# A mixed stack of attention and expert layers on one core: values of the local layers by DRAM, norm factors on GpSimd, heads scored side by side

## The reference, cut to what matters

```python
def attn_layer(x, Wqkv, qs, ksc, Wo):          # x: (16, 256, 128), 16 heads of 64
    q, k, v = jnp.split(x @ Wqkv, 3, -1)        # per head
    q = l2norm(q) * qs
    k = l2norm(k) * ksc
    q = q * cos * scale + rotate_half(q) * sin * scale
    k = k * cos * inv + rotate_half(k) * sin * inv
    out = local_attention(q, k, v)              # windows of 32 see themselves and the one before
    return out @ Wo
def ffn_layer(x, g, bln, W1, b1, W2, b2):
    a, gate = jnp.split((layernorm(x) * g + bln) @ W1 + b1, 2, -1)
    return a * gelu(gate) @ W2 + b2
for i in range(6):
    x = attn_layer(shift_tokens(x), ...) + x
    x = ffn_layer(shift_tokens(x), ...) + x
```

## Time and profile before

| | us |
|---|---|
| median of three runs | 7244.83 (7240.41 to 7246.15) |
| the profiled execution | 7247.5 |
| its span | 7245.8 |
| TensorE busy | 6522.4 (90%) |
| VectorE busy | 4927.7 (68%) |
| ScalarE busy | 4182.4 (58%) |
| GpSimd busy | 2901.3 (40%) |

### The profile page before, as it was taken

One profiled execution on the slowest core, in us unless ns is written; L12 is line 12 of the kernel. 1 busy time (PEld: TensorE's weight loads), 2 busy tenths in 40 slices (PEclk: granted clock), 3 DMA queues, 4 the chain that ended last, 5 costly groups with the idle time before them and its releaser, 6 DMA issues. The chain is left out here.

```text
span 7245.8 us, 217809 instructions
## 1 busy us (share of the span) xinstructions
PE 6522.4 (90%) x79314; PEld 4468.9 (62%) x79314; DVE 4927.7 (68%) x14182; ACT 4182.4 (58%) x10030; POOL 2901.3 (40%) x2911
## 2 busy tenths in 40 slices
PE   7999979999988888888888888888888888879998
PEld 5777657776655565555555556555555555557676
DVE  4555535555657777777777777777777777668378
ACT  4666637776224655656655665565665566446355
POOL 0000010000004666666666666666666666530030
PEclk9999989999989999999999999999999999979999
DMA  1000000000000000000000000000000000010210
GB/s 34 24 25 25 23 27 29 28 28 22 10 33 20 23 4 5 23 4 5 5 23 5 4 5 22 5 5 4 23 5 4 23 4 5 5 37 16 81 38 24
DMA packets 131939, 133.17 MB, mean 18 GB/s; under 512 B 40302, under 2 KB 121982, under 8 KB 130814
## 3 DMA queue, kind: packets, MB, share of 16 engines
q1 hardware_dynamic: 115454, 103.45, 4.4%
q0 software_dynamic: 7936, 24.28, 1.1%
q10 hardware_dynamic: 8448, 4.20, 0.2%
HBM read 55.48 MB, written 10.49 MB: 9 GB/s over the span
## 5 line engine op out<-in xcount | busy, mean ns | idle before, releaser
L937 POOL TENSOR_TENSOR l_rot<-l_rot,l_by_sin 128x512 f32<-128x512 f32 x768 | 961.1, 1272 | 438.6 <-DVE l_by_sin L1301 424.5
L944 POOL TENSOR_TENSOR l_rot<-l_rot,l_norms 128x512 f32<-128x512 f32 x768 | 793.7, 1064 | 485.0 <-DVE l_norms L1322 485.0
L1019 PE MATMUL bank<-w_w,l_x 128*128 (+1 forms) x1536 | 802.0, 631 | 133.8 <-DVE l_by_sin L1301 126.3
L1198 ACT ACTIVATE l_squares<-bank 128x512 f32<-128x512 f32 x768 | 447.5, 596 | 518.9 <-DVE l_square_sums L1306 491.8
L1025 PE MATMUL bank<-w_w,l_x_windows 128*128 (+1 forms) x1536 | 721.0, 602 | 0.0
L1297 DVE TENSOR_TENSOR l_rot<-bank,l_cos 128x512 f32<-128x512 f32 x768 | 519.2, 676 | 295.7 <-ACT l_squares L1198 294.4
L486 PE MATMUL bank<-a_qk 64*128 64x256 f32 (+2 forms) x2660 | 679.5, 381 | 6.1 <-DVE a_qk L668 3.5
L402 POOL DMA_DIRECT2D a_w<-in_a x23 | 13.0, 565 | 1554.2 <-PE bank L514 1431.0
L593 ACT ACTIVATE a_probs_t<-bank 128x512 f32<-128x512 f32 (+1 forms) x656 | 355.9, 554 | 353.7 <-PE bank L494 353.7
L1219 ACT ACTIVATE l_probs_t<-bank 128x512 f32<-128x512 f32 x384 | 208.7, 595 | 598.2 <-PE bank L1061 598.2
L1035 PE MATMUL bank<-ident,l_rot 128*128 128x128 f32 x3072 | 476.4, 283 | 74.3 <-ACT l_probs_t L1219 48.0
(11 more groups left out here) (265 smaller groups left out, 14415.8 us busy)
## 6 DMA issues: line engine op xcount, KB each, us to landing
a_x<-normed_t SPq DMA_DIRECT2D x320, 128.0 KB, 2.0
l_stage_rows<-inner SPq DMA_DIRECT2D x98, 128.0 KB, 2.1
w_w<-in_w SPq DMA_DIRECT2D x6, 2048.0 KB, 9.5
l_shifted_half<-inner SPq DMA_DIRECT2D x98, 63.5 KB
f_w<-in_f SPq DMA_DIRECT2D x9, 514.5 KB, 3.2
a_w<-in_a POOLq DMA_DIRECT2D x18, 256.0 KB, 2.9
f_w<-in_f POOLq DMA_DIRECT2D x9, 512.0 KB, 4.4
c_x<-normed_t SPq DMA_DIRECT2D x36, 128.0 KB, 2.0
```

What stands on the lines that cost most here:

```text
L937: nc.gpsimd.tensor_tensor(rot[s][n][:], rot[s][n][:], by_sin[n % 2][:], ALU.add).then_inc(summed, 1)
L944: nc.gpsimd.tensor_tensor(mine, mine, along(norms[s][:, 8 * n:8 * n + 8], HD), ALU.mult)\
L1019: nc.tensor.matmul(rows_p[i][:], x[:, W + i * P:W + (i + 1) * P], layer_w(layer, quad * QUAD, QUAD), start=True, stop=True).then_inc(rows_ ...
L1198: nc.scalar.activation(squares[i][:], rows_p[i][:], ACT.Square).then_inc(squared, 1)
```

## The change

In `attention` the two heads of an item are turned first and then scored, one after the other. In `local_layers`:

- The values are projected in two tiles of 128 tokens instead of four windows; ScalarE copies them to `v_rows`, SP stores these in a DRAM buffer with 32 zero rows in front (`store_v`) and, once the half's `weigh` is over, loads the windows back in four transfers (`load_v`). `copy_window` and `x_windows` go.
- `norm_factors` moves from VectorE to GpSimd. The step that VectorE did in one operation with two functions takes two there: 14 dependent operations of 128x32.
- The FFN is shifted: `ups` is the next iteration's second product, `hide_rows` follows the maxima of the first half, `give` and `add_ffn` come in the second half, `row_stats(g + 1)` and `deviations(g + 1)` too, `normalise_rows` at the top. The FFN's weights load in two parts.
- ScalarE runs one-element Exp and Gelu operations at the top of an iteration and after the second half's exponentials, and the squares of the next iteration's first part at the end.

```diff
                 def item(quad, p, buffers, b, gp):
                     k, now = quad * 4 + p, buffers[0]
                         pass_heads = range(pass_, min(pass_ + 2, heads))
                         for j in pass_heads:
                             turn(k, p, j)
-                            if by_turns:
-                                scores(k + 1, p + 1, j)
-                        if not by_turns:
-                            for j in pass_heads:
-                                scores(k + 1, p + 1, j)
+                        for j in pass_heads:
+                            scores(k + 1, p + 1, j)
                         for j in pass_heads:
                             weigh(k, p, j)
 
...
+                def store_v(u, o, fill):
+                    for i in range(2):
+                        sp.wait_ge(t_freed[i], fill + 1)
+                        sp.sem_inc(begun, 1)
+                    sp.dma_start(v_dram[o][W:, :].rearrange("(i p) n -> p i n", p=P), v_rows[:]).then_inc(v_stored, DMA)
+
+                def load_v(u, o):
+                    sp.wait_ge(v_stored, (u + 1) * DMA)
+                    sp.sem_inc(begun, 1)
+                    for i in range(2):
+                        for s in range(2):
+                            at = i * P + s * W
+                            sp.dma_start(v[HD * i + W * s:HD * i + W * (s + 1), :, o * QUAD:(o + 1) * QUAD],
+                                         v_dram[o][at:at + P, :].rearrange("(j c) n -> c j n", c=W)).then_inc(v_loaded[o], DMA)
+
+                def iteration(g, L=None, last=False):
...
                     stage_x(g + 2)
...
+                    if not last:
+                        send_v(g, 0)
                     sp.wait_ge(normed, g + 1)
                     sp.sem_inc(begun, 1)
                     sp.wait_ge(added, g + 2)
                     sp.sem_inc(begun, 1)
                     shift((g + NB - 1) & (NB - 1))
...
+                    if not last:
+                        send_v(g, 1)
...
+                def send_v(g, o):
+
+                    h = 2 * g + o
+                    sp.wait_ge(v_loaded[o], (g + 1) * 4 * DMA)
+                    sp.sem_inc(begun, 1)
+                    store_v(h + 2, o, t_fill(h))
+                    sp.wait_ge(heads_filled, 4 * h + 4)
+                    sp.sem_inc(begun, 1)
+                    load_v(h + 2, o)
...
+                def norm_factors(u, s):
+
+                    link = chain(pool, newton, 14 * u)
+                    guess = norms[s]
+                    pool.wait_ge(reduced, 4 * u + 4)
+                    pool.sem_inc(begun, 1)
+                    link(nc.gpsimd.tensor_scalar(minus_half_x[:], square_sums[s][:], 1e-24, -0.5, ALU.max, ALU.mult))
+                    pool.sem_inc(begun, 1)
+                    link(nc.gpsimd.tensor_scalar(guess[:].bitcast(I32), minus_half_x[:].bitcast(I32), -0.5,
+                                                 float(0x5F3759DF - (1 << 30) - (1 << 22)), ALU.mult, ALU.add))
+                    for n in range(3):
+                        link(nc.gpsimd.tensor_tensor(step[:], guess[:], guess[:], ALU.mult))
+                        link(nc.gpsimd.tensor_tensor(step[:], step[:], minus_half_x[:], ALU.mult))
+                        link(nc.gpsimd.tensor_tensor(step[:], step[:], three_halves[:], ALU.add))
+                        link(nc.gpsimd.tensor_tensor(guess[:], guess[:], step[:], ALU.mult))
+
                 def norm(u, s):
-                    pool.wait_ge(newton, 11 * (u + 1))
+                    norm_factors(u, s)
+                    pool.wait_ge(newton, 14 * (u + 1))
...
-                def copy_window(f):
-                    pool.wait_ge(x_moved, f + 1)
...
                             add_sin(h + 2, o, 0)
                         subtract_best(h)
                         weight(h)
-                        if o == 0:
-                            deviations(g)
+                        if o == 1:
+                            deviations(g + 1)
                         if not last:
                             add_sin(h + 2, o, 1)
-                            if o == 0:
-                                for bank in range(2):
-                                    pool.wait_ge(t_filled[bank], 20 * g + 12)
-                                copy_window(g + 1)
                             norm(h + 2, o)
...
                 def project_v(o, fill, layer):
-                    for j in range(4):
-                        reached(pe, t_freed[j % 2], fill + j // 2)
-                        nc.tensor.matmul(t_p[j % 2][:], x_windows[:, j].rearrange("p t s c -> p (t s c)"),
-                                         layer_w(layer, wv_at + o * QUAD, QUAD), start=True, stop=True)\
-                            .then_inc(t_filled[j % 2], 2)
+                    for i in range(2):
+                        reached(pe, t_freed[i], fill)
+                        nc.tensor.matmul(t_p[i][:], x[:, tile_of(i)], layer_w(layer, wv_at + o * QUAD, QUAD), start=True,
+                                         stop=True).then_inc(t_filled[i], 2)
...
+                    pe.wait_ge(v_loaded[o], ((h >> 1) + 1) * 4 * DMA)
...
                             project_rows(h + 2, o, 0, (g + 1) >> 4)
+                        if o == 0:
+                            ups(g)
+                        else:
+                            give(g)
                         scores(h, o)
                         if not last:
                             project_rows(h + 2, o, 1, (g + 1) >> 4)
+                            project_v(o, fill, (g + 1) >> 4)
                         if o == 0:
-                            project_v(1, fill, g >> 4)
                             output(g)
-                            give(g)
-                        elif more:
-                            pe.wait_ge(window_ready, g + 2)
-                            project_v(0, fill, (g + 1) >> 4)
-                            turn_x(g + 2, 3 * g + 2)
-                        if o == 1:
+                        else:
+                            if not last:
+                                turn_x(g + 2, 3 * g + 3)
                             gates(g)
                         turn_probs(h, turned)
                         if more:
-                            turn_qk(h + 1, 1 - o, fill + 3)
+                            turn_qk(h + 1, 1 - o, turned + 1)
                         if o == 0:
                             turn_normed(g)
                         weigh(h, o, turned)
-                        if o == 1:
-                            ups(g)
...
-                def iteration(g, last=False):
+                def iteration(g, last=False, squared_next=True):
+
+                    nc.scalar.activation(warm[:], core.ones[:, 0:1], ACT.Exp)
                     for o in range(2):
                         h = 2 * g + o
-                        fill, more = t_fill(h), o == 0 or not last
+                        fill = t_fill(h)
+                        turned = fill if last else fill + 1
                         if not last:
-                            square(h + 2, 0)
+                            if o == 1:
+                                square(h + 2, 0)
                             square(h + 2, 1)
-                        if more:
-                            move_v(1 - o, 0, fill)
-                            move_v(1 - o, 1, fill)
-                        exps(h, 0)
-                        if more:
-                            move_v(1 - o, 2, fill)
-                        exps(h, 1)
-                        if more:
-                            move_v(1 - o, 3, fill)
-                        if o == 1 and not last:
-                            move_x(g + 2, f_fill(g) + 1)
-                        move_probs(fill + 2 if more else fill)
-                        if more:
-                            move_qk(1 - o, fill + 3)
+                        if o == 0:
+                            exps(h, 0)
+                            if not last:
+                                move_v(h + 2, 0, fill)
+                            exps(h, 1)
+                            if not last:
+                                move_v(h + 2, 1, fill)
+                        else:
+                            if not last:
+                                move_v(h + 2, 0, fill)
+                                move_v(h + 2, 1, fill)
+                            exps(h, 0)
+                            if not last:
+                                move_x(g + 2, f_fill(g) + 2)
+                            exps(h, 1)
+                            nc.scalar.activation(warm[:], core.ones[:, 0:1], ACT.Gelu)
+                        move_probs(turned)
+                        if o == 0 or not last:
+                            move_qk(1 - o, turned + 1)
                         if o == 0:
                             move_normed(g)
                         else:
                             open_gates(g)
```

(22 more changed lines are left out.)

195 lines of the change are left out of this document (115 added, 80 removed).

## The result

| | before | after |
|---|---|---|
| median of four runs each | 7242.62 us (7238.74 to 7246.15) | 7084.16 us (7082.84 to 7087.73) |
| ratio to before, 95% interval | 1 | 0.9782 (0.977 to 0.9794) |
| span of the profiled execution | 7245.8 us | 7081.7 us |
| first issue of the local stage's rows | 2241.5 | 2159.5 |
| last issue of them | 6275.3 | 6108.4 |

The forecast was 6900 us; the kernel gave 158 us instead of 344. The last two lines split the 164 us by which the profiled spans differ. Both kernels issue the load of the stage's rows 98 times, in about 96 periods. So the two attentions gave 2241.5 - 2159.5 = **82 us** (forecast 73), the local stage 4033.8 - 3948.9 = **85 us** (forecast 276), and 3 us were lost at the ends (forecast 5). A local iteration went from 4033.8/96 = 42.0 to 3948.9/96 = **41.1 us**, not to 39.2. The whole miss lies there.

What follows compares the result with a forecast made beforehand. TensorE was taken to carry the local iteration (42.1 us), with GpSimd setting the pace afterwards. Local stage 276 plus attentions 73, less 5 lost at the ends, gave 344 us off 7247.5: about 6900 us, range 6690 to 7160.

Steps and rivals of the forecast that it cites:

- the moved loads of shifted rows: Local stage, second half (R its start): shifted rows behind value loads land R+6.9 to R+9.5, costing 0.4 us an iteration.
- rival B: Local stage: shifted rows landing 12 us into the second half cost 3.1 us an iteration, 7156 us; chance 0.15.
- GpSimd sets the pace: Local stage: GpSimd's chain, with the norm factors added, becomes the longest path at 38.8 us an iteration.
- The other path: Local stage: TensorE's work of 33.9 us plus its remaining waits comes to 37.1 us an iteration, below GpSimd's chain.
- The 0.84 goes: Local stage: TensorE's 0.84 us wait for the Gelu disappears, its table load running beside the probabilities' round trip.
- Rival D: Local stage: GpSimd is cheap, 0.27 us a link, and TensorE's path decides at 37.1 us, 6700 us; chance 0.15.
- The values: Local stage: projecting two tiles saves TensorE 3.75 us an iteration, leaving 33.9; the values' store and reload stay hidden.
- The norm factors: Local stage: VectorE loses 5.0 us an iteration; GpSimd gains 28 links of 0.33 us, 9.2 us.
- Heads side by side: Two-head attentions: both heads' scores overlap on TensorE; items of 5.67 and 5.13 us, saving 73 us together.
- Rival C: Two-head attentions: the heads do not overlap in the loop, 151 us lost, 7124 us; chance 0.07.
- rival A: Local stage: GpSimd's norm-factor links are dearer, 0.48 us each, making it slower than before, 7299 us; chance 0.10.
- E: The forecast itself: a GpSimd norm-factor link of 0.30 to 0.37 us, 6785 to 7025 us; chance 0.53.

Runs made afterwards that it cites:

- the run that gave it all the room: Changed kernel with shifted rows ahead of the value loads and one Newton step instead of three in the norm factors: 6844.25 us, ratio 0.9451.

## Why the prediction was right in its sign and wrong in its size

**The step that failed is the moved loads of shifted rows.** The mechanism stood there and in rival B; the size was off. I had the values moved by R+5.7, the rows landed at R+6.9 if beside them and R+9.5 if after, took 0 to 0.6 us, and chose 0.4. Measured: the values took until about R+6, the rows moved after them, at 15 GB/s and not at the 17 to 18 of the earlier trace rows (by which their 63.5 KB take 4.3 us in place of 3.75), landed at R+11.1, some 5 us behind the end of the values' traffic, and cost 41.1 - 39.4 = **1.7 us an iteration, 164 us in all**. A charge of 0.4 x 95 = 38 us became 164: 126 of the 191 us missed in the local stage. Two errors were one: I set the upper bound by the row's duration when nothing else is on the queues, and I took a value between two cases where the question was which of the two holds. The Trainium skill's rule that stood beside rival B (DMA: Bandwidth & Descriptors, one engine for 127 partitions, in ring order) named the case that holds, as the run with 112 and 15 rows showed; I let it move neither the bound nor the charge. What came in its place is rival B, to which I had given a chance of 0.15. Its price was too high as well: it priced a landing at R+12 at 3.1 us, all that goes beyond R+8.9, by which R+11.1 would cost 2.2; the runs say 1.7. With the rows early GpSimd still waits 1.37 us ahead of the second weighting and not the forced 0.70, so a part of the delay would have been there anyway.

**GpSimd sets the pace: right; 38.8 us: 0.6 too low.** With the late rows cured the period is 39.4. The link was right (0.33 against 0.325 measured), and so was the first half, 18.8 us by my terms and 18.86 in the trace. Within it two errors cancel: a chain of 14 takes 4.9 us instead of 4.6 (4023.05 to 4027.93), its first operation and its two waits being longer, and the normalisation 4.04 instead of 4.23. The second half of the run with early rows takes 39.4 - 18.9 = 20.5 us for my 20.0: the subtraction takes 2.24 instead of 2.04, and up to 1.37 instead of 0.70 us go by ahead of the weighting. That is some 0.6 us an iteration, 58 us.

**The rest of the local stage's miss**, 191 - 126 - 58 = 7 us, lies in the periods taken (42.1 x 95 against 42.0 x 96).

**The other path, 37.1 us: wrong, and it decided nothing.** It is 38.7. "The 0.84 goes" was true of the Gelu, and the output products then waited 1.44 us for the hidden rows. Rival D at 6700 us could therefore not have come about: the run that gave it all the room ended at 6844. That the wait ahead of the gate products is for the copy of x was my reading; the trace only says "issue".

**The values: right as far as tested.** TensorE keeps 3097/3740 x 41.1 = 34.1 us of work an iteration, at a granted clock of 0.98 (forecast 33.9). With the shifted rows out of the way the store and the reload are still made, and the period is that of GpSimd's chain, so they are hidden. No run leaves them out.

**The norm factors: their cost right, their worth not asked.** I charged GpSimd 9.2 us and credited VectorE's 5.0 us with nothing. The runs put the move at 152 us with early shifted rows and 297 with late ones.

**Heads side by side: right.** 5.66 and 5.09 us an item for 5.67 and 5.13, 82 us for 73, and 87 as a change of its own. The mechanism is in the rows too: the second turn waits for VectorE's probabilities, which I had made the longer chain. Rival C had no part, rival A neither.

**The range** reached to B for just this case, so that the time, between E and B, lies in it. That is no credit to the forecast: 158 us came where 344 were forecast.

## The kernels that beat both

With the whole computation, 6913.32 us (statistics behind the sums), ratio 0.9545: one call moved down three lines. With two Newton steps, early shifted rows and the hidden rows between the maxima, 6781.56 us, ratio 0.9363; its norm factors are coarser by the step left out.

## What to carry to other kernels

When an edit puts a transfer behind others, ask first by how many engines it moves and then what stands behind its wait on the waiting engine; a slow transfer of 64 KB behind a fast one of a megabyte cost 1.7 us of each 39, and sending it in another shape, sending it earlier or waiting for it later each took that back whole. When two cases give different prices, decide between them; a value in between belongs to neither. Before an edit is called a gain, find the path that takes over (here 38.7 us behind 39.4): an edit on it is worth nothing until the first one is short enough, as the hidden rows showed with 68 us on one side and nothing on the other.

## What the runs showed of the hardware

- The issue of the one row left over (0.2 KB), right behind the transfer of the 127, held SP for 4.91 us behind the four value loads and 2.71 us ahead of them. With the 127 rows sent as 112 and 15, the issue of the 15 took 0.96 us and that of the one row 0.64.
- The 127 rows moved at 15 GB/s behind the values, at 0.08 of the 16 DMA engines, and took a stretch to themselves; the values moved at over 200.
- A VectorE tensor_scalar of 128x64 took 0.30 us once GpSimd's products of 128x512 had ended and 1.08 beside them.
- An operation on 128x32 in a chain on GpSimd costs 0.325 us from start to start (0.24 to 0.25 busy), on VectorE 0.226.
- The scores of two heads, on rows 0 to 63 and 64 to 127, take 1.14 us (eight records, so four products); those of one head 1.13 (four records).
- TensorE's granted clock in the middle of the local stage was 1.00 before and 0.98 after, and 1.00 again with two Newton steps, where TensorE waits less; with the factors on VectorE it was 0.94 with late shifted rows and 0.99 with early ones.
